# Edge products on one Trainium2 core: where two tiles of the middle block are summed, and where the last block's sums are cleared

## The reference, cut to what matters

```python
def _L1_gnn_ref(x_nodes, x_edges, path_coeffs, src, dst, path_indices):
    x1 = x_nodes[src].reshape(-1, N_SEG, EXTENT)        # N_SEG 16, EXTENT 32
    x2 = x_edges.reshape(-1, N_SEG, EXTENT)
    i1, i2, i3 = (path_indices[:, 0], path_indices[:, 1], path_indices[:, 2])
    contrib = path_coeffs[None, :, None] * x1[:, i1, :] * x2[:, i2, :]
    edge_out = jnp.zeros((x2.shape[0], N_SEG, EXTENT)).at[:, i3, :].add(contrib)
    return jnp.zeros((n_nodes, OP_SIZE)).at[dst].add(edge_out.reshape(-1, OP_SIZE))
```

## Time and profile before

| | us |
|---|---|
| median of 3 runs | 276.04 (275.96 to 276.04) |
| the profiled execution's own time | 276.05 |
| its span in the profile | 274.2 |
| block 1, from DVE's first multiply to its last add | 125.5 to 182.1 |
| block 2, to DVE's last add | 182.1 to 225.6 |

### The profile page before, as it was taken

How to read it: one execution, slowest core, us unless ns; L and a number is a source line. 1 busy time by engine, 2 the same in 40 slices (tenths; PEclk the granted TensorE clock), 3 DMA queues, 4 the chain that set the end, 5 groups by cost and what they waited for, 6 DMA issues and landing times.

```text
span 274.2 us, 5661 instructions
## 1 busy us (share of the span) xinstructions
PE 262.2 (96%) x1631; PEld 185.1 (67%) x1639; DVE 223.6 (82%) x662; ACT 168.5 (61%) x341; POOL 39.5 (14%) x52
## 2 busy tenths in 40 slices
PE   6899999999999899998999999989999989999996
PEld 4566798886444799996778786756665654478633
DVE  5977665299657999999999999999999987755272
ACT  6931341010526999978878787499999709443260
POOL 4000150060006766661000000000000000000000
PEclk9999999999999999999999999999999999999999
DMA  6699990000014765555342000014544439000002
GB/s 208 222 414 409 436 421 17 0 4 0 1 38 127 200 176 152 157 154 155 88 145 77 2 1 1 2 28 145 161 154 150 151 89 343 31 2 2 2 0 76
DMA packets 12592, 33.91 MB, mean 124 GB/s; under 512 B 3345, under 2 KB 3602, under 8 KB 12306
## 3 DMA queue, kind: packets, MB, share of 16 engines
q1 hardware_dynamic: 10482, 26.73, 27.1%
q0 software_dynamic: 2080, 6.82, 8.8%
HBM read 32.50 MB, written 1.05 MB: 122 GB/s over the span
## 4 chain that ended last, share of the span: by engine, by line
PE 83%; DVE 9%; issue 3%; ACT 2%; DVEq 1%; DMA 1%; ACTq 0%; SPq 0%
PE psum L1349 15%; PE psum L1296 14%; PE psum L1250 10%; PE psum L1352 8%; PE psum L1274 5%; DVE big L1041 4%; PE psum L1279 4%; PE psum L1302 3%; PE psum L1423 3%; PE psum L1449 3%; PE psum L1193 3%; PE psum L1179 2%; PE psum L1133 2%; PE psum L1340 1%; PE psum L1231 1%
## 5 line engine op out<-in xcount | busy, mean ns | idle before, releaser
L1296 PE MATMUL psum<-big,dst_oh 128*128 128x512 f32 x108 | 50.7, 594 | 0.5 <-DVE big L1041 0.5
L607 ACT ACTIVATE prod<-edges,coef_b 128x320 f32 (+1 forms) x78 | 43.8, 594 | 10.6 <-PE psum L1352 9.2
L1349 PE MATMUL psum<-prod,ident 128*128 128x128 f32 x160 | 32.1, 295 | 1.0 <-DVE prod L1031 0.9
L1349 PEld LDWEIGHTS psum<-prod,ident 128*128 128x128 f32 x160 | 24.5, 190 | 10.2 <-issue 9.4
L1031 DVE TENSOR_TENSOR prod<-big,prod 128x320 f32<-128x320 f32 (+1 forms) x53 | 29.1, 551 | 0.5 <-issue 0.3
L1296 PEld LDWEIGHTS psum<-big,dst_oh 128*128 128x128 f32 x108 | 18.7, 191 | 15.1 <-issue 14.3
L1250 PE MATMUL psum<-edges,big 128*128 128x256 f32 x128 | 28.3, 380 | 0.0
L607 ACT ACTIVATE xparts<-edges,coef_b 128x320 f32 (+1 forms) x48 | 26.1, 589 | 1.0 <-PE psum L1349 0.6
L1250 PEld LDWEIGHTS psum<-edges,big 128*128 128x128 f32 x128 | 24.1, 190 | 3.5 <-issue 0.3
L1041 DVE TENSOR_TENSOR big<-big,prod 128x64 f32 (+2 forms) x80 | 26.3, 329 | 0.0
L472 POOL DMA_INDIRECT big<-xn_rows,big x16 | 16.9, 1059 | 30.5 <-DMA xn_rows<-xn 23.5
(11 more groups left out here) (221 smaller groups left out, 525.1 us busy)
## 6 DMA issues: line engine op xcount, KB each, us to landing
big<-in_w SPq DMA_DIRECT2D x3, 2048.0 KB, 16.0
edges<-in_edge SPq DMA_DIRECT2D x1, 3584.0 KB, 23.9
edges<-in_f SPq DMA_DIRECT2D x7, 512.0 KB, 3.5
edges<-in_edge SPq DMA_DIRECT2D x1, 2560.0 KB, 23.4
edges<-in_edge SPq DMA_DIRECT2D x5, 512.0 KB, 3.6
edges<-in_f SPq DMA_DIRECT2D x1, 2560.0 KB, 9.8
big<-in_f SPq DMA_DIRECT2D x4, 512.0 KB, 3.6
big<-in_gnn_w SPq DMA_DIRECT2D x1, 1024.0 KB, 6.0
```

What stands on the lines that cost most here:

```text
L607: nc.scalar.activation(slot(n)[:, 0:BLOCKS[b], :], segment(edges_of(b), single_column(words, p)), ACT.Copy, scale=coef_b[:, p:p + 1]).then ...
L1296: last = mm(bank[2 + h], dst_oh[:, n % DR, h * P:(h + 1) * P], tile_sums(b, t), start=False, stop=False)
L1349: last = mm(path_sums(to), ident[:], product[:, 0:PT].rearrange("p t u -> p (t u)"), start=False, stop=True, skip_group_check=True)
```

## The change

Two things are done, and the places of some buffers and waits follow from them.

1. In block 1 two more tiles (the first two of the eight that DVE adds) are summed by PE for the first 28 paths (MID), in banks 2 and 3, with one more 64-column identity matmul in each of these paths. DVE's add has 192 columns instead of 256 there. PE clears banks 2 and 3 at the block's start, once all eight copies of block 0's sums are made. ACT copies both banks to the two tiles' places in SBUF (`copy_mid`) ahead of its scale of path 39; DVE's add of path 28 and PE's first scatter wait for that (`mid_out`). The scatters of block 0 now stand behind paths 29, 32, 35, 38, 41, 45, 48, 51, 54 and 57. The filling matmul L1356 is left out behind path 28. From path 27 of block 1 on, DVE multiplies three steps ahead of its add instead of one (MID_AHEAD).
2. Block 2's sums lie in `x1g[0]`, and ACT clears the six tiles one at a time ahead of its scale of paths 20, 26, 32, 38, 44 and 50 of block 1. The clearing at block 2's start and its wait are gone. `ctrl` and the part of `f1` are loaded to `sum_room[0]`, with a further wait for block 0's scatters.

```diff
-        kept_sums = [sum_room[0][:, 0:KEPT[0], :], x1g[1][:, 0:KEPT[1], :], sum_room[0][:, 0:KEPT[2], :]]
-        rest_sums = [sum_room[0][:, KEPT[0]:, :], sum_room[1], sum_room[0][:, KEPT[2]:, :]]
+        kept_sums = [sum_room[0][:, 0:KEPT[0], :], x1g[1][:, 0:KEPT[1], :], x1g[0][:, 0:KEPT[2], :]]
+        rest_sums = [sum_room[0][:, KEPT[0]:, :], sum_room[1], x1g[0][:, KEPT[2]:BLOCKS[2], :]]
...
             n = BLOCKS[b - 1] - EARLY[b] if b else 0
-            return [-1] * EARLY[b] + [1 + i * (NP - 4) // n for i in range(n)]
+            lo = MID + 1 if b == 1 else 1
+            return [-1] * EARLY[b] + [lo + i * (NP - 3 - lo) // n for i in range(n)]
...
+            def copy_mid():
+
+                act.wait_ge(psums, NP + MID)
+                for i in range(2):
+                    nc.scalar.activation(
+                        rest_sums[1][:, 0:MID_TILES, i * D // 2:(i + 1) * D // 2].rearrange("p t (k u) -> p k t u", u=U),
+                        bank[2 + i].rearrange("p (k t u) -> p k t u", t=MID_TILES, u=U), ACT.Copy).then_inc(mid_out, 1)
...
-                if b == 2 and p == 0:
-                    act.wait_ge(scattered, FIRST[1])
-                    for i in range(BLOCKS[b] - KEPT[b]):
-                        nc.scalar.activation(rest_sums[b][:, i, :], zero_b[:, 0:1].broadcast_to([P, D]), ACT.Copy)\
-                            .then_inc(cleared[b], 1)
+                if b == 1 and p == MID + SLOTS - 1:
+                    copy_mid()
+                if b == 1 and (p - CLEAR_AT) % CLEAR_EVERY == 0 and 0 <= p - CLEAR_AT < CLEAR_EVERY * (BLOCKS[2] - KEPT[2]):
+
+                    act.wait_ge(mults, NP)
+                    nc.scalar.activation(rest_sums[2][:, (p - CLEAR_AT) // CLEAR_EVERY, :], zero_b[:, 0:1].broadcast_to([P, D]), ACT.Copy)\
+                        .then_inc(cleared[2], 1)
...
+                if n == NP + MID:
+                    dve.wait_ge(mid_out, 2)
+                lo = MID_TILES if b == 1 and p < MID else 0
+                v = segment(rest_sums[b][:, lo:, :], out_column(words[b], p))
+                nc.vector.tensor_tensor(v, v, slot(n)[:, KEPT[b] + lo:BLOCKS[b], :], ALU.add).then_inc(sums, 1)
...
             for n in range(NP * NB):
-                if n + 1 < NP * NB:
-                    multiply(n + 1)
+                ahead = n + (MID_AHEAD if n >= NP + MID - 1 else 1)
+                while multiplied < min(ahead, NP * NB - 1):
+                    multiplied += 1
+                    multiply(multiplied)
                 add(n)
...
                 if n == 0:
-
+                    pe.wait_ge(mid_out, 2)
                     for h in range(H):
                         mm(bank[2 + h], ident[:], xs[:, h, :], start=True, stop=False)
...
+                for q in (2, 3) if b == 1 else ():
+                    pe.wait_ge(block_out, banks_before(1))
+                    mm(bank[q], zero_b[:], dst_ohb[:, 0:2, :].rearrange("p t n -> p (t n)"), start=True, stop=True)
...
+                    if b == 1 and p < MID:
+                        last = mm(mid_sums(to), ident[:],
+                                  product[:, KEPT[b]:KEPT[b] + MID_TILES].rearrange("p t u -> p (t u)"),
+                                  start=False, stop=True, skip_group_check=True)
                     last.then_inc(psums, 1)
-                    if KEPT[b] > PT and b and p % 2 and p < NP - 1:
+                    if b == 1 and p < MID and p % 2:
                         mm(bank[4][:, 0:N], zero_b[:], iota_b, start=False, stop=True, skip_group_check=True)
```

More of the change, by code:

```diff
@@ L42, in graph_and_experts @@
     PT = 4
+    MID, MID_TILES, MID_AHEAD = 28, 2, 3
     PE_TILES = 8
@@ L59, in graph_and_experts @@
     FREE_SLOTS = 2
+    CLEAR_AT, CLEAR_EVERY = 20, 6
     SPLIT = 7
@@ L87, in more_sums, with mid_sums @@
             return product_sums(psum[:, 0:NS * PT2[b] * U], PT2[b] * U, k)
+        def mid_sums(k):
+            return product_sums(psum[:, 2 * 512:4 * 512], MID_TILES * U, k)
         def carve(base, dt_size=4):
@@ L217, in graph_and_experts @@
         w_cat = take([KC, G + EX])
-        take = carve(x1g[0].rearrange("p t f -> p (t f)"))
+        take = carve(sum_room[0].rearrange("p t f -> p (t f)"))
         f1_parts = [take([KC // 2, f1.shape[1]])]
@@ L224, in graph_and_experts @@
         f2_hi = carve(late)([FC - 6, D])
-        take = carve(big[:, BLOCKS[0] * D:])
+        take = carve(big[:, 0:(BLOCKS[0] + 2 * BLOCKS[1] - KEPT[1]) * D])
         xnT2 = take([KC, N])
@@ L357, in graph_and_experts @@
         block_out = sem("block_out")
+        mid_out = sem("mid_out")
         scattered, x3_ready = sem("scattered"), sem("x3_ready")
@@ L416, in _ @@
             sp.wait_ge(mults, NP * (NB - 1))
+            sp.wait_ge(scattered, FIRST[1])
             sp.dma_start(ctrl_sb, rows(ctrl)).then_inc(ctrl_in, 16)
@@ L994, in _ @@
                         .then_inc(part_r, 1)
-            nc.vector.memset(rest_sums[1][:, 0:4, :], 0.0).then_inc(cleared[1], 1)
+            nc.vector.memset(rest_sums[1][:, MID_TILES:4, :], 0.0).then_inc(cleared[1], 1)
             dve.wait_ge(packed, 3)
@@ L1039, in add @@
                     dve.wait_ge(sums, n)
-                v = segment(rest_sums[b], out_column(words[b], p))
-                nc.vector.tensor_tensor(v, v, slot(n)[:, KEPT[b]:BLOCKS[b], :], ALU.add).then_inc(sums, 1)
+                if n == NP + MID:
[3 more added lines that the diff above has]
+                nc.vector.tensor_tensor(v, v, slot(n)[:, KEPT[b] + lo:BLOCKS[b], :], ALU.add).then_inc(sums, 1)
             multiply(0)
+            multiplied = 0
             for n in range(NP * NB):
-                if n + 1 < NP * NB:
-                    multiply(n + 1)
+                ahead = n + (MID_AHEAD if n >= NP + MID - 1 else 1)
+                while multiplied < min(ahead, NP * NB - 1):
+                    multiplied += 1
+                    multiply(multiplied)
                 add(n)
```

## The result

The changed kernel takes **281.75 us** (median of 4 runs, 280.60 to 282.69) against 276.03 (4 runs beside it, 275.96 to 276.04): ratio **1.0205**, 95% interval 1.0182 to 1.0229. The sign was forecast; the size was not. 279.2 was said, with a range up to 281.2. The four runs lie in two pairs: 280.60 and 280.88 with a mean granted clock of 1.000 over the span, 282.63 and 282.69 with 0.994. The first pair lies inside the stated range, the second above it; the median lies between the pairs, where no run is.

A forecast was written before the change was run, and what follows sets the result against it. DVE was taken to set the pace, with PE nearly as full. The terms -1.9 + 1.0 + 3.5 + 0.5 gave +3.1 us on the profiled 276.05, so 279.2 us, range 277.2 to 281.2.

The forecast's parts named there:

- Bound: Block 1 and block 2: DVE sets the pace, PE nearly as full; each microsecond saved on DVE counts until others delay it.
- Part 1: Block 1's first 28 paths: DVE's adds of 192 columns instead of 256 save 28 x 0.067, -1.9 us.
- Part 2: Start of block 2: removing ACT's clearing is worth 0.2 us, between 0 and 0.99.
- Part 3: PE up to path 27 of block 1: 0.21 us per added matmul (0.11 to 0.22), path 27 done at 150.0.
- Part 4: Middle of block 1: DVE's add of path 28 waits for two bank copies, +1.0 us (0 to 1.5).
- Part 5: PE's rest of block 1: x copy, ten scatters, 34 paths without filler take 33.3 us, ending at 184.8.
- Part 6: Block 1's end: ACT's late copies make DVE's multiply of path 6 of block 2 wait, +3.5 us.
- Part 7: Kernel's end: last three adds run without a multiply between, +0.5 us; what follows is unchanged and moves along.
- The first: Rival: narrow matmuls cost by their columns, PE ends block 1 at 180.2, both waits vanish; 274.5 us, chance 0.08 for faster.
- The second: Rival: the lead absorbs most of PE's late end, boundary wait 1 instead of 3.5 us; about 276.5, chance 0.08.
- The third: Rival: the delay feeds on itself through ACT's scales in block 2, another 1.5 to 2.5 us; 281.5, chance 0.12.
- The fourth: Rival: removing the clearing frees more than seen, at most DVE's free 0.99 us in block 2; chance 0.02.

The follow-up runs named there:

- experiment 2: Changed kernel plus 14 filling matmuls on PE behind the last path, ahead of the wait for the last adds: 280.58 to 280.61 us.
- experiment 5: Kernel before with only the moved clearing (block 2's sums in x1g[0], cleared during block 1): median 275.85 us, ratio 0.9990.
- experiment 9: Changed kernel without its 14 filling matmuls in block 1's first 28 paths: 279.92 to 279.93 us at full clock, 281.62 at 0.994.
- experiment 3: Changed kernel with ACT's copies of block 1's banks behind path 10 of block 2 instead of path 5: 279.08 to 279.09 us at full clock, 280.65 at 0.994.
- experiment 6: Kernel before with the moved clearing and block 0's scatters deferred behind paths 29 to 57, without added matmul, middle copies or lead: 280.45 to 280.48 us.
- experiment 7: Changed kernel with 20 paths instead of 28, scatters from path 21: 278.23 us at full clock, 279.89 to 279.94 at 0.994.
- experiment 1: Changed kernel with DVE back to one multiply ahead from the start of block 2: 279.43 to 279.52 us.
- experiment 10: Kernel before with DVE multiplying three steps ahead in its last 20 steps: 276.56 to 276.90 us in six runs, 278.04 to 278.50 in six.
- experiment 8: Changed kernel with 20 paths, five multiplies ahead until block 1 ends and one afterwards, ACT's copies behind path 10: 276.99 to 277.08 us, ratio 1.0035.
- experiment 11: Kernel before with the moved clearing and three filling matmuls between PE's last path and the last scatters: 275.86 to 276.29 us, ratio 0.9986.
- experiment 4: Changed kernel with block 0's scatters adding to the first half of the nodes only: 280.31 and 279.02 us, clock 0.982 and 0.988.

## Why the prediction was right in its sign and wrong in its size

The forecast of 279.2 misses twice. At the full clock the change takes 280.6, 1.4 above it and still within its range; that is sizes of terms. The clock puts the median outside the range; that is a step which the forecast did not have. By its own parts, with 280.6 (experiment 2) as what the parts 1 to 6 and the first half of part 7 should give:

- **Bound.** Right. DVE set the pace, and each wait of it came out in the time.
- **Part 1, the shorter adds, -1.9.** Right: the adds of 192 columns stand at a pace of 0.80 to 0.81, and that is all that the change gains.
- **Part 2, the clearing, -0.2.** Right as far as it can be told: -0.17, within the noise, and -0.22 in the trace (experiment 5).
- **Part 3, PE's price.** Mis-sized. I took the average of a pair, 0.21, and charged the filler 0.11. The named upper end, 0.22, was the price of every 4-byte matmul (experiment 9), and the filler's share is 0.05. PE's 28th path ended near 150.6 in the profiled execution and 150.3 in experiment 2's, not 150.0. The Trainium skill (TensorE: Matmul & The Clock Gate, "LDWEIGHTS (loading the stationary operand)") lets a weight load go by its own columns; the runs agree with the forecast's choice of that over a price by moving columns: a 4-byte matmul with 128 stationary columns costs 0.223 for 64 and for 128 moving ones (experiment 9).
- **Part 4, the middle wait, +1.0.** It was 1.5, the upper bound, by part 3 and, as the trace reads, by ACT: PE's 28th path ends at about 150.6 and the copies start at 151.05, since a clearing call of 0.5 us stands ahead of ACT's scale of path 38. I had moved that call without placing it. That share was not tested by itself.
- **Part 5, PE's second part, 33.3 us.** It took 152.25 to 186.50, 34.25. The rows give 24 paths at 0.45, ten behind a scatter at 0.39, and ten scatters and the copy of x at about 1.77, together 34.2. Here too the filler that is removed saved next to nothing.
- **Part 6, the block's end, +3.5.** Mechanism right (experiments 3, 6 and 7), size 4.13 - 0.2 = 3.9. I gave the upper bound 1.0 more, and 0.4 came. (With the bounds named, the upper end of the sum is +4.6, not the +4.7 that I wrote.)
- **Part 7, the end.** Its +0.5 was right, three adds 0.54 apart. Its last sentence, "What follows is unchanged and moves along", is **the step that failed**. It costed the row of adds on DVE and didn't ask what PE does meanwhile. PE is without work for 1.3 us, and in half of the runs the granted clock then falls to 0.50 under the next scatters: +1.7 to 1.9 us (experiments 1, 2 and 10).
- **Rivals.** The first fell on the 0.22. The second fell: the copies wait for PE. The third, that the delay feeds on itself, did not come by its mechanism. Block 2 adds only waits of 0.2, and the rest of its time is the clock, so that its 281.5 lies near the measured median is luck. The fourth kept its bound: the clearing gave 0.2.

The sum with measured terms is -1.9 - 0.2 + 1.5 + 4.1 + 0.5 = +4.0; the last add came 4.5 later in experiment 2's trace (229.83 against 225.29). Of the remaining 0.5, the two waits without a releaser (0.20 and 0.18, where before had one of 0.19) are 0.2. The rest is on the side of the work: in experiment 2's trace DVE is idle for 6.65 us between block 1's start and the last add, against 0.65 before, and busy for 98.09 against 99.55, 1.5 less and not 1.9. With the clock's part in half of the runs the median falls between the two groups.

What stays open: why a gap of 1.3 us is followed by the lower clock in half of the executions and not in all. The runs show how often, and that with the gap short or filled a fall there is rare. They don't show what decides it in one execution.

## What to carry to other kernels

Work taken from the bounding engine is gained only if the work that must make room for it doesn't end later. Here ten scatters lost 28 paths of room for 1.9 us of adds, and the deferral alone cost 4.6 us at the next block's start, through a copy that stands at a fixed place in a third engine's order. Price moved work by the stretch it is moved into, and look what every engine does while a newly serial piece runs: a 1.3 us gap of TensorE ahead of its heaviest matmuls cost more than the serial adds themselves, and with 14 fillers in it (experiment 2) or without the serial adds (experiment 1) no run had the lower clock.

## What the runs showed of the hardware that I had not expected

- A filling bf16 matmul of 256 columns between 4-byte matmuls adds 0.05 to 0.06 us to a pair of paths, though its start-to-start time reads 0.11; the matmul ahead of it is shorter by the difference.
- With a gap of TensorE of 1.3 us ahead of the last scatters, 13 of 28 runs had a lower mean clock (the change 2 of 4, experiments 3, 7 and 9 together 5 of 12, experiment 10 6 of 12). With the gap short or filled, in experiments 1, 2, 6, 8 and 11, none of 28 runs had it, in experiment 5 one of 11, and of the kernel before 3 of 46. These runs took 1.4 to 2.5 us longer than the median of the same kernel's runs at the full clock; only that of experiment 5 took no longer. That the fall lies behind the gap is seen in the traces of the change and of experiments 4, 7 and 10; of the runs without a trace it is inferred from their times.
- A fall lasted 3.4 us in these traces and began up to 1 us after TensorE had started again. In experiment 4 another began while TensorE stood still and lasted 6.8 us, and in experiment 10 another followed a wait of only 0.26 us.
- An add of DVE that waits for the add directly ahead of it starts 0.54 us behind it at the end of the kernel, and 0.60 behind it at the start of block 2 in experiment 8. With an independent multiply between, an add lengthens the row by 0.27.
